# Keys and values of a fused attention layer: the fifth products on half the rows each, and weight chunks issued ahead of the turning transfers

## The chip, the cores and the metric

One core of one Trainium2 chip runs the whole kernel. The metric is the device time of one execution in microseconds; lower is better. A core has five instruction streams that matter here: TensorE (PE in the profile, with its weight loads as PEld), VectorE (DVE), ScalarE (ACT), GpSimd (POOL) and SyncE (SP), which here only issues DMA transfers. They meet at semaphores.

## The reference, cut to what matters

```
h  = tokenizer(x)                      # sines and cosines times W, joined with txt: 8 batches x 640 rows x 192
xn = layernorm(h)
k  = xn @ Wk ; v = xn @ Wv             # 192 -> 12 heads x 64
kf = concat(relu(k), relu(-k))         # per head, 128 features
kv = einsum('bhnd,bhnm->bhdm', kf, v)  # per batch and head, summed over the 640 rows
...                                    # queries, attention with kv, fusing product Wf (3072 x 768), Wo
h  = h + attention ; h = h + soft_experts(layernorm(h))
```

Every float32 product is built from bfloat16 halves: a value is its high half plus its low half, and a product is high by high, high by low and low by high.

## The kernel before, in words

The program runs in five stages, each a block with an end at which all engines meet: `tokenizer`, `attention_weights`, `keys_and_values`, `attend`, `soft_experts`. The change lies in the class `KeyInputs`, in `attention_weights` and `keys_and_values`, and with one transfer in `attend`.

The 5,120 rows of h are 40 tiles of 128 rows, 5 to a batch. For each tile, DVE normalizes 192 columns (L349), ACT copies the high half to `x_halves` (L353), DVE subtracts for the low half in two instructions (L356 and L357), and SP turns the three blocks of 128 columns by one DMA transpose into a slot of `x_turned` (L362). The blocks are: columns 0 to 127 high; columns 128 to 191 high over their low half; columns 0 to 127 low. So block 1 holds two things in its 128 rows: rows 0 to 63 are the high half of the last 64 columns, rows 64 to 127 their low half. The weights hold the last 64 rows of Wk and Wv twice, in rows 0 to 63 and 64 to 127.

`keys_and_values` makes, for each tile and each half of the heads (`hf`), keys and values of 384 columns each, by five matmuls for keys and then five for values (L642 to L646), into two banks. The fifth, L646, multiplies block 1 by the low weights. The last one of values releases ACT, which takes the positive part (L691), the negative part (L692) and the high half of values (L693). DVE and POOL subtract for the low halves of the features (L738 on DVE, L785 on POOL), DVE for the low half of values (L741). PE then adds 18 small matmuls (L658, six heads by three) to the sums `ps_kv`. PE's order is written out: project half hf of tile t, then accumulate half hf of tile t-1. `project` waits for L692 and L741 of the same half one tile earlier; `accumulate` waits for L738, L785, L693 and L741 of its half.

The stage also splits the 24 chunks of the fusing weights Wf, three to a batch, in tiles t = 0, 1 and 2. A chunk is loaded by SP (L596) into one of two buffers of `ex_big`. ACT makes its high half (L715) after both halves of its tile's key features; POOL makes the low half in two pieces (L791), each behind the L785 of the same hf, and waits for L715 with the first. So in these tiles L785 of hf = 1 comes after L715. Chunks 0 and 2 of a batch use buffer 0, chunk 1 uses buffer 1; a load waits until POOL is through with the chunk before it in the buffer.

SP's queue is in order. In iteration n (tile n, t = n mod 5) it stores tile n+1 of `x_turned` to memory (`keep_x`, L611), then turns tile n+3 (`turn_x`, L362), which waits for the low half L357 that DVE makes at the end of tile n, and then loads: at t = 1 chunk 2 of this batch, at t = 4 chunks 0 and 1 of the next.

`attend` begins with some 20 small loads for the last stage (L1010 to L1024, counted by `ex_in`), reads the kept tiles (L999, L1000) and turns its outputs (L1031). DVE adds the bias `bf` at the end of each tile (L1257). `bf` is loaded by ACT in `attention_weights` (L415).

Of the kernel before, what the change touches and what calls it, by code (L numbers as in the profile page):

```python
# [6 lines left out]
F32 = mybir.dt.float32  # L7
# [318 lines left out]
class KeyInputs:  # L326
# [3 lines left out]

    LEAD = 3
# [3 lines left out]
    def __init__(self, nc, sb, sem, xn):  # L335
        self.nc = nc
        self.xn = xn
        self.xs = sb("x_halves", [P, 2, 3 * P], BF16)
        self.xt = sb("x_turned", [P, 4, 3, P], BF16)
        self.norm, self.high, self.low, self.kept = (sem("x_" + n) for n in ("norm", "high", "low", "kept"))  # L340
        self.turned = [sem(f"x_turned{n}") for n in range(4)]
# [10 lines left out]
    def high_half(self, x):  # L352
        self.nc.scalar.activation(self.xs[:, x, 0:DIM], self.xn[:, :], ACT.Copy).then_inc(self.high, 1)  # L353

    def low_half(self, x):
        self.nc.vector.tensor_tensor(self.xs[:, x, 2 * P:3 * P], self.xn[:, 0:P], self.xs[:, x, 0:P], ALU.subtract)  # L356
        self.nc.vector.tensor_tensor(self.xs[:, x, DIM:2 * P], self.xn[:, P:DIM], self.xs[:, x, P:DIM],  # L357
                                     ALU.subtract).then_inc(self.low, 1)
# [6 lines left out]
def attention_weights(nc, a, w, wq_t, kv_f, x, stats, h, ident):  # L365
# [6 lines left out]
    with ExitStack() as ctx:  # L372
# [23 lines left out]
        with nc.Block() as block:  # L396
            @block.sync
            def _(sp):
                sp.dma_start(wt[:, :, :], a['wt_diag']).then_inc(wt_in, 16)
                sp.dma_start(bias[TAIL:P, :], a['bias_rows']).then_inc(bias_in, 16)  # L400
                sp.dma_start(wo_f[:, :, :], a['wo']).then_inc(wo_in, 16)
                for n in range(x.LEAD):
                    sp.wait_ge(x.low, n + 1)
                    x.turn(sp, n)
                for n in range(x.LEAD):
                    sp.wait_ge(x.turned[n], 16)

            @block.scalar
            def _(act):
# [5 lines left out]
                act.dma_start(w['bf'][:, :], a['bf'].partition_broadcast(P)).then_inc(small_in, 16)  # L415
# [26 lines left out]
                act.wait_ge(small_in, 16 * 8)  # L442

            @block.gpsimd
            def _(pool):
# [10 lines left out]
                eps = w['eps'][:, 0:PART]  # L456
                nc.gpsimd.memset(w['half'][:, :], -0.5).then_inc(halved, 1)  # L457
# [26 lines left out]
            def _(dve):  # L484
# [39 lines left out]
                dve.wait_ge(small_in, 16 * 8)  # L524
# [5 lines left out]
def keys_and_values(nc, a, w, x, x_kept, wf_f, kv_hi, kv_lo, stats, h, ident):  # L530
# [11 lines left out]
    with ExitStack() as ctx:  # L542
# [46 lines left out]
        with nc.Block() as block:  # L589
            @block.sync  # L590
            def _(sp):
# [14 lines left out]
                def keep_x(n):  # L606
                    at, uses = x.place(n // x.PERIOD, n % x.PERIOD)
                    sp.wait_ge(x.turned[at], 16 * uses + 16)
                    if n:
                        sp.wait_ge(x.kept, 16 * n)  # L610
                    sp.dma_start(x_kept[n], x.xt[:, at].rearrange("p k n -> p (k n)")).then_inc(x.kept, 16)  # L611
# [18 lines left out]
            def _(pe):  # L630
                def project(b, t, hf, early):
# [7 lines left out]
                    for kv in range(2):  # L639
                        cols = slice(kv * INNER + hf * HC, kv * INNER + (hf + 1) * HC)  # L640
                        out = ps_p[:, hf, kv, 0:HC]
                        nc.tensor.matmul(out, x.xt[:, at, 0], w['kv_hi'][:, 0, cols], start=True, stop=False)  # L642
                        nc.tensor.matmul(out, x.xt[:, at, 0], w['kv_lo'][:, 0, cols], start=False, stop=False)
                        nc.tensor.matmul(out, x.xt[:, at, 2], w['kv_hi'][:, 0, cols], start=False, stop=False)
                        nc.tensor.matmul(out, x.xt[:, at, 1], w['kv_hi'][:, 1, cols], start=False, stop=False)
                        last = nc.tensor.matmul(out, x.xt[:, at, 1], w['kv_lo'][:, 1, cols], start=False, stop=True)  # L646
# [154 lines left out]
def expert_tiles(sb):  # L801

# [42 lines left out]
def attend(nc, a, ex, w, x_kept, shared, kv_hi, kv_lo, h, ident):  # L845
# [14 lines left out]
    with ExitStack() as ctx:  # L860
# [66 lines left out]
        def count(tile, k, n):  # L927

            return n * tile.t + k + 1
# [62 lines left out]
        with nc.Block() as block:  # L992
            @block.sync
            def _(sp):
# [208 lines left out]
            def _(dve):  # L1203
# [49 lines left out]
                def move_y(tile):  # L1253
                    dve.wait_ge(s["fused"], count(tile, NO - 1, NO))
# [30 lines left out]
                def slots_square():  # L1285
                    dve.wait_ge(s["ex_in"], 16 * 20)
# [634 lines left out]
def early_fusion_kernel(nc, a, out):  # L1921
    with ExitStack() as ctx:
# [14 lines left out]
        with ExitStack() as attn:  # L1937
            def sa(name, shape, dt):
                return attn.enter_context(nc.sbuf_tensor(name, shape, dt))
# [5 lines left out]
                 'betaf': sa("betaf", [P, INNER // P], F32), 'bf': sa("bf", [P, INNER], F32),  # L1945
# [8 lines left out]
            with ExitStack() as keys:  # L1954
                x = KeyInputs(nc, lambda *v: keys.enter_context(nc.sbuf_tensor(*v)),
                              lambda name: keys.enter_context(nc.semaphore(name)), ex['xn'])
# [73 lines left out]
```

## Time and profile before

| | |
|---|---|
| time, median of 3 runs | 2398.43 us (2396.47 to 2402.49) |
| the profiled execution: its own time | 2402.28 us |
| its span, first to last instruction | 2400.6 us |
| mean granted TensorE clock | 0.977 |
| tokenizer | 0 to about 470 us |
| attention_weights | about 470 to 505.6 us |
| keys_and_values | 505.6 to about 722.6 us |
| attend | about 723 to 2340 us |
| soft_experts | the rest |

Busy time of PE counts each matmul from its start to its modelled end. Matmuls overlap: one of 384 columns is shown with 326 ns and the next one starts 162 ns after it, so the distance between starts is PE's pace. The clock column is the granted TensorE clock as a share of full speed.

### The profile page before, as it was taken

Reading aid. Unit: us, or ns where it says so; the run is one execution under the profiler, and the core shown is the slowest. Engines: PE = TensorE matmul, PEld = TensorE weight load, DVE = VectorE, ACT = ScalarE, POOL = GpSimd, SP = SyncE. Lnnn points to the kernel's source line nnn. Section 1 sums busy time; section 2 is a strip of 40 time slices with the busy share of each in tenths; the row PEclk is TensorE's granted clock in tenths of the full one; section 3 lists DMA queues with packets and bytes.
Section 4 is the critical chain, followed back from the end, with each engine's and each line's share of the span. In section 5 each row is a group of like instructions: output and inputs, shape, how many; then the busy total and the mean of one; then the engine's idle time right before and its main releaser. Section 6 shows DMA issues by size and latency. Waiting matters only on the chain. (4 is left out here: it accounts for less than half of the span.)

```text
span 2400.6 us, 58403 instructions
## 1 busy us (share of the span) xinstructions
PE 2270.0 (95%) x20906; PEld 1552.0 (65%) x20906; DVE 1998.1 (83%) x3021; ACT 1836.3 (76%) x2812; POOL 1286.2 (54%) x1253
## 2 busy tenths in 40 slices
PE   5999999978887999999999999999999999999976
PEld 3777777655554666666666666666666666666654
DVE  7999999876767888888888888888888888888855
ACT  6767677556667888888888888888888888888853
POOL 0000000056666776777777767676767767676760
PEclk9999999989998999999999999999999999999987
DMA  6412111122322222222222222222222222222212
GB/s 148 132 41 56 43 39 39 36 60 76 85 71 37 45 41 43 41 43 41 43 42 44 43 44 43 41 43 41 43 41 43 42 45 43 43 41 43 42 32 67
DMA packets 306607, 121.75 MB, mean 51 GB/s; under 512 B 280244, under 2 KB 297140, under 8 KB 306228
## 3 DMA queue, kind: packets, MB, share of 16 engines
q1 hardware_dynamic: 305396, 120.47, 23.4%
q8 instruction: 36, 0.59, 0.1%
q10 hardware_dynamic: 1152, 0.51, 0.1%
q14 instruction: 23, 0.19, 0.0%
HBM read 46.21 MB, written 7.86 MB: 23 GB/s over the span
## 5 line engine op out<-in xcount | busy, mean ns | idle before, releaser
L1162 ACT ACTIVATE phi<-ps_t,betat,gt 64x512 f32<-64x512 f32 (+1 forms) x1280 | 851.8, 665 | 17.4 <-PE ps_t L1061 0.2
L1093 PE MATMUL ps_y<-staging,o_turned 128*128 128x384 bf16 x3840 | 820.5, 326 | 0.0
L1377 POOL TENSOR_TENSOR phi_lo<-phi 128x512 bf16<-128x512 f32 x480 | 504.2, 1051 | 442.4 <-ACT phi L1162 442.4
L1093 PEld LDWEIGHTS ps_y<-staging,o_turned 128*128 128x128 bf16 x3840 | 361.8, 98 | 218.8 <-issue 0.2
L1093 PE MATMUL ps_y<-wf_lo,o_turned 128*128 128x384 bf16 x1920 | 469.2, 326 | 0.0
L1369 POOL TENSOR_TENSOR q_ssq<-q_ssq,half 128x8 f32<-128x8 f32 x240 | 418.2, 1743 | 18.8
L172 PE MATMUL acc<-w_b,feat 128*128 128x384 bf16 x1728 | 296.2, 331 | 33.1 <-ACT feat L223 27.4
L1250 DVE TENSOR_TENSOR o_halves<-o,o_halves 128x512 bf16<-128x512 f32 x240 | 192.2, 801 | 158.7 <-ACT o_halves L1172 158.6
L1152 ACT ACTIVATE shared<-shared 128x512 f32<-128x512 f32 x240 | 150.1, 626 | 176.6 <-DVE shared L1213 176.1
L1093 PEld LDWEIGHTS ps_y<-wf_lo,o_turned 128*128 128x128 bf16 x1920 | 187.9, 98 | 124.5 <-issue 0.3
L172 PEld LDWEIGHTS acc<-w_b,feat 128*128 128x128 bf16 x1728 | 168.3, 99 | 150.5 <-DVE w_b L298 23.7
L1213 DVE SCALAR_TENSOR_TENSOR shared<-q_sum,shared 128x512 f32<-128x512 f32 x240 | 260.8, 1087 | 1.4
L457 POOL MEMSET half<- 128x40 f32 x1 | 0.1, 131 | 468.7 <-POOLq L112 468.7
L284 DVE TENSOR_TENSOR f_low<-feat 128x4608 bf16<-128x4608 f32 x48 | 237.7, 4951 | 0.0
L1227 DVE TENSOR_TENSOR z<-shared,q_ssq 128x512 f32<-128x512 f32 x240 | 228.1, 950 | 0.6 <-POOL q_ssq L1369 0.6
L1078 PE MATMUL ps_o<-kvs_hi,phi 128*128 (+1 forms) x1920 | 209.0, 194 | 3.6
L1079 PE MATMUL ps_o<-kvs_lo,phi 128*128 (+1 forms) x1920 | 210.6, 194 | 0.0
L1080 PE MATMUL ps_o<-kvs_hi,phi_lo 128*128 (+1 forms) x1920 | 209.5, 193 | 0.0
L210 ACT ACTIVATE near<-xt,fr 128x2304 int32<-128x2304 f32 x48 | 106.6, 2220 | 130.5 <-DVE feat L268 121.9
L1078 PEld LDWEIGHTS ps_o<-kvs_hi,phi 128*128 128x128 bf16 x1920 | 177.7, 98 | 9.3 <-POOL phi_lo L1377 8.4
L1145 ACT ACTIVATE shared<-ps_a 128x512 f32<-128x512 f32 x240 | 143.5, 598 | 50.0 <-PE ps_a L1053 46.2
L1079 PEld LDWEIGHTS ps_o<-kvs_lo,phi 128*128 128x128 bf16 x1920 | 177.6, 98 | 2.8
(255 smaller groups left out, 4689.0 us busy)
## 6 DMA issues: line engine op xcount, KB each, us to landing
xt<-in_x_dram SPq DMA_DIRECT2D x32, 320.0 KB, 4.9
ex_big<-in_wf_dram SPq DMA_DIRECT2D x24, 384.0 KB, 3.6
xt<-in_x_dram SPq DMA_DIRECT2D x32, 256.0 KB, 5.4
x_kept<-x_turned SPq DMA_DIRECT2D x40, 96.0 KB, 2.0
shared<-x_kept SPq DMA_DIRECT2D x40, 96.0 KB, 1.9
o_turned<-o_halves SPq DMA_TRANSPOSE x240, 3.1
out_dram<-h SPq DMA_DIRECT2D x8, 480.0 KB, 5.1
staging<-in_wq_t_dram SPq DMA_DIRECT2D x1, 3072.0 KB, 12.8
```

The source lines that it names most:

```text
L172: last = nc.tensor.matmul(acc[:, u, t, 0:2 * DIM], high(p % RING)[:, k, t * P:(t + 1) * P], w_b[:, i, k, :], start=i == 0 and k == 0, stop ...
L284: nc.vector.tensor_tensor(low[:, r], feat[:, r], high(r), ALU.subtract).then_inc(low_ready, 1)
L1078: nc.tensor.matmul(out, ph, kv_hi[:, b, hd, :], start=c == 0, stop=False, skip_group_check=True)
L1079: nc.tensor.matmul(out, ph, kv_lo[:, b, hd, :], start=False, stop=False, skip_group_check=True)
L1080: last = nc.tensor.matmul(out, pl, kv_hi[:, b, hd, :], start=False, stop=c == PAIRS - 1, skip_group_check=True)
L1093: last = nc.tensor.matmul(ps_y[:, n, 0:HC], lhs, w[part][:, c, n * HC:(n + 1) * HC], start=c == 0 and lhs is hi and part == 'wf_hi', stop= ...
L1162: last = nc.scalar.activation(phi[sign * DH:(sign + 1) * DH, j % 2, a:b, head, :], ps_t[rows, a * P:b * P].rearrange("p (i n) -> p i n", n ...
L1213: nc.vector.scalar_tensor_tensor(out=q[:, j % RING], in0=total[:, j % 2].unsqueeze(2).broadcast_to([P, OCT, DH]), scalar=1.0 / DH, in1=q[: ...
L1227: nc.vector.tensor_tensor(z[:, j % 2], q[:, j % RING], ssq[:, j % 2].unsqueeze(2).broadcast_to([P, OCT, DH]), ALU.mult).then_inc(s["q_scal ...
L1250: nc.vector.tensor_tensor(oh[:, j % 2, 1], o[:, :, :, :].rearrange("p a h d -> p (a h d)"), oh[:, j % 2, 0], ALU.subtract).then_inc(s["o_l ...
L1369: nc.gpsimd.tensor_tensor(ssq[:, j % 2], ssq[:, j % 2], w['half'][:, 0:OCT], ALU.pow).then_inc(s["q_rstd"], 1)
L1377: nc.gpsimd.tensor_tensor(phi_lo[:, j % 2, :, head], phi[:, j % 2, :, head], phi_hi[:, j % 2, :, head], ALU.subtract).then_inc(s["phi_lo_d ...
```

## The change

- The turned input gets a fourth block. ACT writes the high half of the last 64 columns twice, by a second instruction: into the second half of a new block 0 and into the first half of block 2. The first half of block 0 is zero, set once by POOL at the start of `attention_weights`; SP waits for it (`cleared`). The three old blocks are now blocks 1, 2 and 3.
- The fifth product of keys uses rows 0 to 63 only (block 2), that of values rows 64 to 127 only (block 0). Both come after the other eight and stand next to each other in PE's order. The product of low by low half, which the old fifth product had in it, is left out.
- `x_halves` is no buffer of its own any more but lies in the memory of `bf`. So `bf` is loaded in `attend`, by SP, as one more of the loads of `ex_in`, and `move_y` of the first tile waits for it.
- SP loads a chunk of Wf at the start of an iteration, ahead of `keep_x` and `turn_x`: chunk 2 at t = 1, chunk 1 of the next batch at t = 3 and chunk 0 of the next batch at t = 4.

```diff
     def high_half(self, x):
-        self.nc.scalar.activation(self.xs[:, x, 0:DIM], self.xn[:, :], ACT.Copy).then_inc(self.high, 1)
+        self.nc.scalar.activation(self.xs[:, x, P:2 * P], self.xn[:, 0:P], ACT.Copy)
+        twice = self.xs[:, x, TAIL:TAIL + 2 * DIM].rearrange("p (k c) -> p k c", k=2)[:, :, 0:TAIL]
+        self.nc.scalar.activation(twice, self.xn[:, P:DIM].unsqueeze(1).broadcast_to([P, 2, TAIL]),
+                                  ACT.Copy).then_inc(self.high, 1)
...
-        self.xt = sb("x_turned", [P, 4, 3, P], BF16)
+        self.xt = sb("x_turned", [P, 4, 4, P], BF16)
...
+                sp.wait_ge(x.cleared, 1)
...
-                act.dma_start(w['bf'][:, :], a['bf'].partition_broadcast(P)).then_inc(small_in, 16)
...
+                nc.gpsimd.memset(x.xs[:, :, 0:TAIL], 0.0).then_inc(x.cleared, 1)
...
                 for n in range(TILES):
                     b, t = divmod(n, TPB)
+                    if t == 1:
+                        load(PER_BATCH * b + 2)
+                    if t >= 3 and b + 1 < BATCH:
+                        load(PER_BATCH * (b + 1) + 4 - t)
                     if n + 1 < TILES:
                         keep_x(n + 1)
                     if n + x.LEAD < TILES:
                         turn_x(n + x.LEAD)
-                    if t == 1:
-                        load(PER_BATCH * b + 2)
-                    if t == 4 and b + 1 < BATCH:
-                        for k in range(2):
-                            load(PER_BATCH * (b + 1) + k)
...
-                        nc.tensor.matmul(out, x.xt[:, at, 1], w['kv_hi'][:, 1, cols], start=False, stop=False)
-                        last = nc.tensor.matmul(out, x.xt[:, at, 1], w['kv_lo'][:, 1, cols], start=False, stop=True)
+                        nc.tensor.matmul(out, x.xt[:, at, 2], w['kv_hi'][:, 1, cols], start=False, stop=False)
+                    for kv, (rows, block_) in enumerate(((slice(0, TAIL), 2), (slice(TAIL, P), 0))):
+                        cols = slice(kv * INNER + hf * HC, kv * INNER + (hf + 1) * HC)
+                        last = nc.tensor.matmul(ps_p[:, hf, kv, 0:HC], x.xt[rows, at, block_],
+                                                w['kv_lo'][rows, 1, cols], start=False, stop=True)
                     last.then_inc(projected, 1)
...
+                sp.dma_start(w['bf'][:, :], a['bf'].partition_broadcast(P)).then_inc(s["ex_in"], 16)
                 sp.dma_start(ex['scale'][:, :], a['scale'].partition_broadcast(P)).then_inc(s["ex_in"], 16)
-                sp.wait_ge(s["ex_in"], 16 * 20)
+                sp.wait_ge(s["ex_in"], 16 * 21)
...
                 def move_y(tile):
+                    if isinstance(tile.t, int) and tile.t == 0:
+                        dve.wait_ge(s["ex_in"], 16 * 21)
```

## Rows read from the trace of the kernel before

**Rows 1.** Windows, two batches: busy (instructions) of PE, PEld, DVE, ACT, POOL; clock; DMA.
```profile
561.80:590.80 29.00, 23.70 (x280) 15.74 (x279) 17.34 (x37) 16.30 (x41) 15.97 (x17) 0.94 0.28 76
590.80:617.00 26.20, 22.70 (x284) 15.40 (x283) 19.23 (x39) 16.80 (x41) 15.98 (x17) 1.00 0.31 83
```

**Rows 2.** Waits of 505 to 725 us: total us, times, longest.
```profile
ACT kf L691 <- PE ps_p L646: 62.8, 51, 6.4
POOL wf_lo L791 <- ACT staging L715: 59.5, 17, 5.5
PEld ps_kv L658 <- POOL kf_lo L785: 30.1, 16, 3.8
ACT staging L715 <- DMA ex_big<-in_wf_dram: 23.1, 13, 3.0
```

**Rows 3.** Timeline of ACT, one batch.
```profile
589.46 0.49 ACT L691 ACTIVATE kf<-ps_p 128x384 f32<-128x384 f32 x1 [0.90 <-PE ps_p L646]
...
594.50 0.84 ACT L715 ACTIVATE staging<-ex_big 128x768 f32 x1 [1.36 <-DMA ex_big<-in_wf_dram]
...
605.49 0.84 ACT L715 ACTIVATE staging<-ex_big 128x768 f32 x1 [1.73 <-DMA ex_big<-in_wf_dram]
...
615.41 0.49 ACT L691 ACTIVATE kf<-ps_p 128x384 f32<-128x384 f32 x1 [0.68 <-PE ps_p L646]
```

**Rows 4.** Timeline of PE: the first matmuls of two halves.
```profile
562.66 0.33 PE L642 MATMUL ps_p<-shared,x_turned 128*128 128x384 bf16 x1
562.83 0.33 PE L643 MATMUL ps_p<-shared,x_turned 128*128 128x384 bf16 x1
...
564.84 0.33 PE L642 MATMUL ps_p<-shared,x_turned 128*128 128x384 bf16 x1
```

**Rows 5.** Timeline of SP, the same batch as in rows 3.
```profile
584.49 1.19 SPq L362 DMA_TRANSPOSE x_turned<-x_halves  x1
...
590.85 1.04 SPq L596 DMA_DIRECT2D ex_big<-in_wf_dram  x2
...
601.80 0.56 SPq L596 DMA_DIRECT2D ex_big<-in_wf_dram  x1
```

**Rows 6.** Timeline around tile 2 of that batch: POOL, DVE and PE.
```profile
597.52 0.91 POOL L791 TENSOR_TENSOR wf_lo<-ex_big,staging 128x384 f32 x1
...
601.27 1.26 DVE L738 TENSOR_TENSOR kf_lo<-kf 128x384 bf16<-128x384 f32 x1
602.46 0.55 DVE L741 TENSOR_TENSOR v_lo<-ps_p,v_hi 128x384 bf16<-128x384 f32 x1
603.15 0.32 PE L642 MATMUL ps_p<-shared,x_turned 128*128 128x384 bf16 x1 [0.45 <-ACT kf L692]
```

**Rows 7.** Timeline of PE in the last stage, matmuls on 32 rows.
```profile
2376.79 0.24 PE L1886 MATMUL ps_x<-yrows_lo,ct_hi 32*128 32x192 bf16 x2
2376.80 0.25 PE L1886 MATMUL ps_s<-yrows_lo,ct_hi 32*128 32x192 bf16 x2
...
2380.39 0.37 PE L1886 MATMUL ps_s<-yrows_hi,ct_lo 32*128 32x192 bf16 x2
2380.69 0.29 PEld L1865 LDWEIGHTS ps_c<-ex_big,hidden 128*128 128x128 f32 x1 [0.30 <-issue]
```

**Rows 8.** Timeline of ACT in attention_weights: pace of its instructions.
```profile
497.22 0.36 ACT L353 ACTIVATE x_halves<-ex_small 128x192 bf16<-128x192 f32 x1 [1.78 <-DVE ex_small L349]
497.49 0.37 ACT L419 ACTIVATE q_hi<-ps_f 128x256 bf16<-128x256 f32 x1
```

**Rows 9.** DMA issues of the page: KB each, median us to landing.
```profile
ex_big<-in_wf_dram SPq DMA_DIRECT2D x24, 384.0 KB, 3.6
```

**Rows 10.** DMA issues of 505 to 722 us.
```profile
x_turned<-x_halves SPq DMA_TRANSPOSE x37, 2.3
```

**Rows 11.** Timeline of SP at the start of attend.
```profile
734.59 0.42 SPq L1024 DMA_DIRECT2D ex_scale<-in_scale_dram  x1
744.79 0.35 SPq L999 DMA_DIRECT2D shared<-x_kept  x1
```

More of the change, by code:

```diff
@@ L333, with __init__ @@
     PERIOD = len(RING)
-    def __init__(self, nc, sb, sem, xn):
+    def __init__(self, nc, sb, sem, xn, xs):
         self.nc = nc
         self.xn = xn
-        self.xs = sb("x_halves", [P, 2, 3 * P], BF16)
-        self.xt = sb("x_turned", [P, 4, 3, P], BF16)
-        self.norm, self.high, self.low, self.kept = (sem("x_" + n) for n in ("norm", "high", "low", "kept"))
+        self.xs = xs
+        self.xt = sb("x_turned", [P, 4, 4, P], BF16)
+        self.norm, self.high, self.low, self.kept, self.cleared = (
+            sem("x_" + n) for n in ("norm", "high", "low", "kept", "cleared"))
         self.turned = [sem(f"x_turned{n}") for n in range(4)]
@@ L441, in _ @@
                         nc.scalar.activation(w['wo_hi'][:, :, :], wo_f[:, :, :], ACT.Copy).then_inc(wo_hi_done, 1)
-                act.wait_ge(small_in, 16 * 8)
+                act.wait_ge(small_in, 16 * 7)
             @block.gpsimd
@@ L522, in _ @@
                                                 ALU.subtract).then_inc(bias_split, 1)
-                dve.wait_ge(small_in, 16 * 8)
+                dve.wait_ge(small_in, 16 * 7)
                 for n, sign in (('gt', 0), ('betat', 1)):
@@ L610, in keep_x @@
                         sp.wait_ge(x.kept, 16 * n)
-                    sp.dma_start(x_kept[n], x.xt[:, at].rearrange("p k n -> p (k n)")).then_inc(x.kept, 16)
+                    sp.dma_start(x_kept[n], x.xt[:, at, 1:4].rearrange("p k n -> p (k n)")).then_inc(x.kept, 16)
                 load(0)
@@ L641, in project @@
                         out = ps_p[:, hf, kv, 0:HC]
-                        nc.tensor.matmul(out, x.xt[:, at, 0], w['kv_hi'][:, 0, cols], start=True, stop=False)
-                        nc.tensor.matmul(out, x.xt[:, at, 0], w['kv_lo'][:, 0, cols], start=False, stop=False)
-                        nc.tensor.matmul(out, x.xt[:, at, 2], w['kv_hi'][:, 0, cols], start=False, stop=False)
-                        nc.tensor.matmul(out, x.xt[:, at, 1], w['kv_hi'][:, 1, cols], start=False, stop=False)
-                        last = nc.tensor.matmul(out, x.xt[:, at, 1], w['kv_lo'][:, 1, cols], start=False, stop=True)
+                        nc.tensor.matmul(out, x.xt[:, at, 1], w['kv_hi'][:, 0, cols], start=True, stop=False)
+                        nc.tensor.matmul(out, x.xt[:, at, 1], w['kv_lo'][:, 0, cols], start=False, stop=False)
+                        nc.tensor.matmul(out, x.xt[:, at, 3], w['kv_hi'][:, 0, cols], start=False, stop=False)
+                        nc.tensor.matmul(out, x.xt[:, at, 2], w['kv_hi'][:, 1, cols], start=False, stop=False)
[3 more added lines that the diff above has]
+                                                w['kv_lo'][rows, 1, cols], start=False, stop=True)
                     last.then_inc(projected, 1)
@@ L1285, in slots_square @@
                 def slots_square():
-                    dve.wait_ge(s["ex_in"], 16 * 20)
+                    dve.wait_ge(s["ex_in"], 16 * 21)
                     nc.vector.tensor_tensor(ex['sl_sq'][:, :, :], ex['sl'][:, :, :], ex['sl'][:, :, :],
@@ L1955, in early_fusion_kernel @@
                 x = KeyInputs(nc, lambda *v: keys.enter_context(nc.sbuf_tensor(*v)),
-                              lambda name: keys.enter_context(nc.semaphore(name)), ex['xn'])
+                              lambda name: keys.enter_context(nc.semaphore(name)), ex['xn'],
+                              w['bf'].bitcast(BF16)[:, 0:8 * P].rearrange("p (k c) -> p k c", k=2))
                 attention_weights(nc, a, w, wq_t, kv_f, x, stats, h, ident)
```

6 lines of the change are left out of this document (3 added, 3 removed).

## The prediction

> **What bounds the kernel now.** I read the page first: PE is busy nearly everywhere, and the stage `keys_and_values` is one of the few stretches where its digits drop. It takes 217 us (505.6 to 722.6), 27 us a batch. The windows by batch then show that no engine is full there: in an undisturbed batch of 26.2 us PE is busy 22.7, DVE 19.2, ACT 16.8, POOL 16.0, at full clock [rows 1]. So the stage is held by waits. The rows of PE give its own need: one half of a tile takes 562.66 to 564.84, 2.18 us, made of ten matmuls at about 162 ns and 18 small ones for 0.56 us [rows 4]. Ten halves are 21.8 us; a batch takes 25.95 from its first L691 to that of the next [rows 3]. So some 4.2 us a batch are lost to waits.
>
> The list of waits names the chain [rows 2]. ACT waits 23.1 us in 13 waits for chunks of Wf. POOL waits 59.5 us for L715, the ACT copy of a chunk. PE's loads for L658 wait 30.1 us for POOL's L785, which stands behind that copy in POOL's order. The ACT waits for PE (62.8 us) are its normal slack; PE has none of that kind. The timeline shows where the loads come late. ACT wants chunk 0 at 593.14 and gets it at 594.50; it wants chunk 2 at 603.76 and gets it at 605.49 [rows 3]. SP had issued them at 590.85 and 601.80, each some 3.7 us before its use [rows 3, 5], and 3.6 us is what such a load takes [rows 9]. In SP's queue they stand behind a turning transfer that waits for the end of the tile.
>
> A second limit sits behind it. In tile 2 DVE's L738 takes 1.26 us, L741 of the same size 0.55; POOL, which works at the same time, is the likely reason. So the low half of values is done at 603.01 (602.46 plus 0.55), and PE starts its next half at 603.15 after 0.45 us of idle time [rows 6]. The row names L692 there, but L741 is the other wait of `project` and ended last. No load has to do with these 0.45 us.
>
> **The change part by part.**
>
> *Loads ahead.* Chunk 0 of a batch now goes out at the start of iteration t = 4, right behind the turning transfer of t = 3: that ended at 585.68 (584.49 plus 1.19), against 590.85 [rows 5]. Five microseconds earlier where 1.4 are missing: the wait goes. Chunk 1 goes two tiles before its use: it stays hidden. Chunk 2 is the thin one. It moves to the start of iteration t = 1, but must wait for POOL's second piece of chunk 0, which ended at 598.43 (597.52 plus 0.91), 3.1 us after ACT's copy of chunk 0 (594.50 plus 0.84) [rows 3, 6]. With the copy 1.4 us earlier that is 597.1; plus 3.7 is 600.8. ACT will want it at about 601.7 (603.76 less the 1.4 and some 0.7 of faster pace) [rows 3]. Hidden with 0.9 us to spare. While SP waits for POOL here, the store and the turn of that iteration stand behind it; the turn waits for the end of tile 1 anyway, which comes later than 597.1. Nothing is late.
>
> Gain: the 23.1 us [rows 2] lie on the path, since POOL's L785 and so PE stand behind them. The long stalls also cost clock: the batch of 29.0 us reads 0.94 instead of 1.00, which is 0.06 x 29 = 1.7 us of PE at full rate [rows 1]. It had the longest wait, 3.0 us [rows 2], and I give 3 us to it and its like. What the wait hid comes out in part: the POOL order (copy, first piece, L785, each about 1 us) leaves PE short some 0.3 to 0.7 us in chunk tiles. I take -25 us, with -18 and -30 as ends.
>
> *Fifth products side by side.* Per half, one slot of 162 ns goes [rows 4] if the two run at the same time. For that the trace has a near row: in the last stage four matmuls on 32 rows each start within 0.01 us and the next four come 0.09 us later, the time of 192 columns once [rows 7]. So 80 x 0.162 = 13 us of PE time. PE sets the pace in some six of the ten halves of a batch; in the chunk tiles DVE and POOL do [rows 6]. I take -7.5 us, ends -13 and, if they don't overlap, 0.
>
> *The border between whole and half array.* Before has no such border with PE busy on both sides at full clock. The nearest: after the last 32-row matmul at 2380.39 the next weight load starts at 2380.69, at half clock, where the matmul itself streams 0.16 [rows 7]. At most 0.14 us, and that includes a semaphore. Lower end 0; upper end per half is two borders at a matmul's tail, 0.326 less 0.162 each, 0.33 us [rows 4]. I take 0.03 per half, half of it on the path: +1 us; upper end +18 (there PE's pace of 2.35 covers the other chains).
>
> The Trainium skill (TensorEngine Tiling (Array Packing), Key Properties) says that a change of the tiling mode drains TensorE, and each half now has two. By that rule the sum is the drain rival below; the last stage's rows lean against it, since that weight load starts before the modelled end of the matmul (2380.39 plus 0.37), but they are one case.
>
> *The doubled high half.* ACT's instruction on 192 columns is followed by the next after 0.27 us [rows 8]. Two of 128 columns take between 0.36 (by columns) and 0.54 (no shorter at all); I take 0.45. That is +0.18 us a tile, 7.2 us of ACT in all. Cover: ACT's waits for PE, 62.8 us [rows 2]. Without cover it is 7.2. In tiles 0 and 1, where a chunk copy and a store of the sums also stand, ACT is nearly full; in `attention_weights` the first three come in a chain. +1 us, ends 0 and +4.
>
> *The fourth block.* The transfer of three blocks lands in 2.3 us [rows 10]; a third more is at most 3.1. It has two tiles until ACT and PE ask for it: nothing, except behind the last of the first three: +0.2. The clearing on POOL and SP's wait for it come long before the first low half: nothing. Storing three of the four blocks moves the same bytes. DVE's two low-half instructions keep their sizes.
>
> *The bias.* ACT issues one load fewer before its first work, when it waits for PE: nothing. SP issues one more, of the size of a chunk's load, behind 734.59. That is 0.6 us and a landing of some 3.6 [rows 9], done by 739; SP next works at 744.79 [rows 11]. Nothing. DVE asks for it at the end of the first tile, far later.
>
> Sum: -25 - 7.5 + 1 + 1 + 0.2 = -30.3 us. The profiled execution took 2402.3 (span 2400.6 plus 1.7), so it would give 2372; the median of the runs is 2398.4, 3.9 lower, and gives **2368**. As a check by batches: PE's own 20.2 us (ten times 2.02) plus some 2.2 of chains (0.4 to 0.7 in each chunk tile [rows 6]) is 22.4; eight of them and the 8 us of start and tail (217 less eight batches of 26.1) are 187 instead of 217. The same 30.
>
> **The rivals.**
>
> *Drain.* Both borders empty the array, +0.33 less 0.162 per half: PE's pace 2.35 us, 23.5 a batch, plus 0.4 of chains; 8 x 23.9 + 8 = 199, 18 us less than 217: **2381**. For it: two borders a half. Against: rows 7.
>
> *One after the other.* The halves don't overlap and the border is free: the loads alone, -25 + 2: **2375**. Against: the side-by-side starts of rows 7, though those are 32-row pieces.
>
> *PE sets the pace throughout.* POOL and DVE keep up: 20.4 a batch, 8 x 20.4 + 8 = 171: -46, **2353**. Against: the slow L738 [rows 6].
>
> *The wait moves.* SP, now waiting for POOL ahead of store and turn, or a chunk 2 that lands late, keeps most of the waits: a gain of 5 to 10 us, **2390**. For it: only 0.9 us to spare.
>
> *Slower.* The fifth products run one after the other and each of the three changes of rows (whole, lower, upper, whole) empties the array and loads its weights in the open: 0.164 plus 0.098 for the load, 0.79 per half. PE's pace is 2.97, a batch 29.7, the stage 246: +29, **2427**. It decides from a loss of 0.4 us per half on, which eats the 30 us of the rest. Against: the weight loads of rows 7 go ahead of the matmuls there.
>
> **How the numbers follow.** Chances: forecast 0.50, drain 0.17, one after the other 0.12, PE throughout 0.10, wait moves 0.06, slower 0.05. A measurement here tells 0.3%, 7.2 us, from no change (the three runs span 6 us). Only the last two cases reach towards no change: part of the wait case gives same. Faster 0.93, same 0.03, slower 0.04. The range holds the forecast with its ends of the load term (-18 and -30), the drain, one after the other, and up to PE throughout: 2352 to 2386, which leaves out the wait case, the slower one and little more.
>
> **What the profile after would show.** Right: no wait of ACT L715 for the transfer, or under 3 us in all; the two fifth matmuls of a half starting within 0.02 us, and the next L658 about 0.16 us later; the distance of first matmuls near 2.02 us in tiles 3 and 4; batches of about 22.4 us with PE's waits for POOL and DVE left in tiles 0 to 2; two ACT instructions 0.22 us apart per tile; the first o_turned transfer as far behind the start of `attend` as now. Drain: the L658 behind the fifth products starts over 0.3 us after them. Wait moves: ACT still waits for chunk 2, or PE for `x_turned`. The prediction is wrong if a batch takes under 21 or over 24.5 us, or if the rest of the kernel moves by more than 3 us.

## The result, and the profile after

The changed kernel took 2384.36 us (median of 4 runs, 2383.16 to 2384.71) beside 2400.46 for the kernel before (4 runs). The ratio is 0.9933, with a 95% interval from 0.9916 to 0.9951. It is faster, but by half of what was forecast: the forecast, 2368 from 2398.4, is a ratio of 0.987. The profiled execution took 2384.16 us, its span is 2382.4, its mean clock 0.979.

The whole gain lies where it was looked for. A clean measure of the stage is the time from the first to the last of its 80 starts of ACT's positive part. Before, it runs from 509.11 to 718.94 us, 209.8 us. After, the first and the last are:

```profile
509.16 0.49 ACT L700 ACTIVATE kf<-ps_p 128x384 f32<-128x384 f32 x1 [6.25 <-PE ps_p L654]
...
700.82 0.49 ACT L700 ACTIVATE kf<-ps_p 128x384 f32<-128x384 f32 x1 [0.97 <-PE ps_p L654]
```

That is 191.7 us, 18.2 less. The rest of the span is the same (2190.8 and 2190.7 us). I call this time **the stage** below. It tells more than the whole time: over all kernels of this study the rest of the span varies between 2186 and 2192 us from one execution to the next, while the stage of the changed kernel, profiled twice, came to 191.7 and 191.1. Every other kernel has one profile, so I read nothing into differences of the stage below 1 us.

The list of waits of the stage after (505 to 706 us; total us, times, longest), the counterpart of [rows 2]:

```profile
ACT kf L700 <- PE ps_p L654: 61.4, 69, 6.3
POOL kf_lo L794 <- ACT kf L701: 41.9, 29, 12.3
POOL wf_lo L800 <- ACT staging L724: 37.7, 22, 3.2
...
PEld ps_p L654 <- issue: 26.0, 80, 0.6
...
PE ps_p L648 <- DVE v_lo L750: 6.2, 5, 1.5
PEld ps_kv L667 <- POOL kf_lo L794: 6.1, 15, 1.2
```

ACT's 23.1 us for the chunks are gone, no such row is left. PE's weight loads wait 6.1 us for POOL instead of 30.1. Two rows are new or larger: the load for the fifth products (L654) stands 0.32 us in each of the 80 halves with nothing to wait for, and PE waits longer for DVE's low half of values (L750). In the kernel before, the same list (505 to 725 us) has for that wait:

```profile
PE ps_p L642 <- DVE v_lo L741: 3.0, 5, 1.7
```

The timeline of SP and of ACT for the same batch as in [rows 3, 5] shows the loads ahead of their use:

```profile
589.56 0.34 SPq L603 DMA_DIRECT2D ex_big<-in_wf_dram  x1
597.47 0.56 SPq L603 DMA_DIRECT2D ex_big<-in_wf_dram  x1
```
```profile
581.74 0.49 ACT L700 ACTIVATE kf<-ps_p 128x384 f32<-128x384 f32 x1 [0.80 <-PE ps_p L654]
...
585.50 0.85 ACT L724 ACTIVATE staging<-ex_big 128x768 f32 x1
...
594.97 0.85 ACT L724 ACTIVATE staging<-ex_big 128x768 f32 x1
...
605.98 0.49 ACT L700 ACTIVATE kf<-ps_p 128x384 f32<-128x384 f32 x1 [0.58 <-PE ps_p L654]
```

Both copies L724, of chunk 0 and of chunk 2, start without a wait. The load at 589.56 is chunk 2 of this batch and the copy at 594.97 its use: 5.4 us, where 3.6 are needed. This batch takes 24.24 us (581.74 to 605.98), where the forecast had 22.4 and had named 24.5 as the point from which it is wrong. The seven distances from batch to batch are 23.5 to 25.3 us, mean 24.46, and three of them are over 24.5; before, they have a mean of 26.35. The windows of two batches (columns as in [rows 1]):

```profile
533.00:556.50 23.50, 22.59 (x287) 13.57 (x284) 17.88 (x37) 17.28 (x46) 16.17 (x16) 1.00 0.53 101
581.70:606.00 24.30, 22.99 (x287) 13.82 (x285) 19.86 (x37) 17.52 (x46) 15.57 (x16) 1.00 0.39 94
```

The clock is at its full level in both. The slower batch has 2 us more of DVE at the same number of instructions (37): DVE's instructions themselves got longer in it.

PE around the fifth products of one half, to be held against [rows 4]:

```profile
589.37 0.32 PE L648 MATMUL ps_p<-shared,x_turned 128*128 128x384 bf16 x1
...
590.34 0.33 PE L650 MATMUL ps_p<-shared,x_turned 128*128 128x384 bf16 x1
590.50 0.33 PE L651 MATMUL ps_p<-shared,x_turned 128*128 128x384 bf16 x1
590.76 0.34 PE L654 MATMUL ps_p<-shared,x_turned 64*128 64x384 bf16 x2
591.03 0.20 PE L667 MATMUL ps_kv<-v_hi,kf 128*128 128x65 bf16 x1
...
591.59 0.33 PE L648 MATMUL ps_p<-shared,x_turned 128*128 128x384 bf16 x1
```
```profile
590.34 0.10 PEld L651 LDWEIGHTS ps_p<-shared,x_turned 128*128 128x128 bf16 x1
590.76 0.10 PEld L654 LDWEIGHTS ps_p<-shared,x_turned 64*128 64x128 bf16 x2 [0.32 <-issue]
591.03 0.10 PEld L667 LDWEIGHTS ps_kv<-v_hi,kf 128*128 128x128 bf16 x1 [0.17 <-issue]
```

The two fifth products do run side by side: one row, x2, 0.34 us, where one matmul alone is shown with 0.33. But from L651 to L654 it is 0.26 us and from L654 to L667 0.27, where a full matmul is followed by the next after 0.16. So each change between whole and half array costs 0.10 us. Two of them are 0.21 us a half; the saved slot is 0.16. A half takes 2.22 us (589.37 to 591.59) instead of 2.18; the forecast had 2.02. The weight loads behave differently too: L651's starts a whole matmul ahead of its own (590.34 for 590.50), L654's and L667's start only with their matmul. What fills the 0.10 us the rows don't settle. An array that empties would look like this, and so would a weight load, itself 0.10 us long, that is no longer hidden behind the matmul before it.

### The profile page after: what moved, and what is told of

It reads as the page before. It is cut to its first block and busy times, and to the rows that moved or that the text cites. A ratio compares the mean times of both kernels' runs of the same rounds, so it can differ in the third digit from the quotient of the medians.

```text
span 2382.4 us, 58446 instructions
## 1 busy us (share of the span) xinstructions
PE 2267.4 (95%) x20906; PEld 1537.5 (65%) x20906; DVE 2006.6 (84%) x3021; ACT 1842.7 (77%) x2852; POOL 1285.5 (54%) x1254
## 3 DMA queue, kind: packets, MB, share of 16 engines
q1 hardware_dynamic: 310660, 122.17, 24.5%
## 5 line engine op out<-in xcount | busy, mean ns | idle before, releaser
L1163 ACT ACTIVATE shared<-shared 128x512 f32<-128x512 f32 x240 | 150.2, 626 | 176.9 <-DVE shared L1224 176.4
L172 PEld LDWEIGHTS acc<-w_b,feat 128*128 128x128 bf16 x1728 | 167.8, 99 | 151.2 <-DVE w_b L298 24.4
```

Of the source, the lines that this page charges most:

```text
L172: last = nc.tensor.matmul(acc[:, u, t, 0:2 * DIM], high(p % RING)[:, k, t * P:(t + 1) * P], w_b[:, i, k, :], start=i == 0 and k == 0, stop ...
```

## The experiments

Each ratio is to the kernel before, run beside it on the same chip, with its 95% interval. "Stage" is the distance defined above; 209.8 before, 191.7 and 191.1 changed. A "half" is the time from one half's first matmul to the next one's where PE waits for nothing.

| kernel | time, us | ratio | stage, us | half, us |
|---|---|---|---|---|
| e1_loads_only | 2380.83 | 0.9925 [0.9911, 0.9938] | 190.9 | 2.18 |
| e2_fifths_only | 2399.30 | 1.0007 [0.9997, 1.0017] | 207.1 | 2.23 |
| e3_whole_fifths | 2381.70 | 0.9925 [0.9912, 0.9939] | 190.6 | 2.18 |
| e4_apart | 2396.69 | 0.9990 [0.9981, 1.0000] | 204.5 | 2.60 |
| e5_pool_order | 2372.88 | 0.9902 [0.9886, 0.9917] | 183.5 | 2.18 |
| e6_no_low_wf | 2362.65 | 0.9861 [0.9846, 0.9876] | 173.5 | 2.18 |
| e7_changed_no_low_wf | 2368.28 | 0.9883 [0.9868, 0.9898] | 176.4 | 2.23 |
| changed_again | 2381.41 | 0.9941 [0.9927, 0.9954] | 191.1 | 2.23 |
| e8_spread | 2378.84 | 0.9921 [0.9907, 0.9934] | 188.3 | 2.18 |
| e9_spread_and_order | 2379.18 | 0.9922 [0.9909, 0.9936] | 187.4 | 2.18 |
| e10_changed_pool_order | 2380.24 | 0.9924 [0.9911, 0.9938] | 188.8 | 2.23 |
| e11_nine_products | 2373.15 | 0.9910 [0.9894, 0.9927] | 183.5 | 2.02 |

### One part of the change at a time

**e1_loads_only** is the kernel before with nothing but the new place of the loads:

```diff
                 for n in range(TILES):
                     b, t = divmod(n, TPB)
+                    if t == 1:
+                        load(PER_BATCH * b + 2)
+                    if t >= 3 and b + 1 < BATCH:
+                        load(PER_BATCH * (b + 1) + 4 - t)
...
-                    if t == 1:
-                        load(PER_BATCH * b + 2)
-                    if t == 4 and b + 1 < BATCH:
-                        for k in range(2):
-                            load(PER_BATCH * (b + 1) + k)
```

> The kernel before with nothing changed but the order of SP's queue (the loads of the Wf chunks ahead of store and turn). Theory (borders): in the changed kernel each border between matmuls on 128 rows and on 64 rows costs PE 0.10 us, so the pair of fifth products saves 0.162 us and costs 0.21, a net loss of 0.05 us per half. Then this run has PE's pace at 2.18 us per half instead of 2.23, batches of some 23.8 us, and ends 1 to 5 us before the changed kernel: 2380 to 2383. Rival (chains): the fifth products gain their 0.162 us and the miss lies in the chains over POOL, DVE and the doubled ACT instruction; then this run is slower than the changed kernel where PE sets the pace: 2388 to 2392.

**e2_fifths_only** is the changed kernel with this edit taken back.

> The changed kernel with SP's queue in the old order (the fifth products, the fourth block, the doubled ACT instruction and the moved bias alone). Borders: PE's pace 2.23 us against 2.18, partly hidden behind the waits for chunks: 2400 to 2405, no faster than before. Chains: 7 us faster than before, 2393.

**e3_whole_fifths** is the changed kernel with its two fifth products in the same place, but on all 128 rows of block 2: no border between whole and half array, nothing side by side, and everything else of the change (fourth block, doubled high half, bias) in it.

```diff
-                    for kv, (rows, block_) in enumerate(((slice(0, TAIL), 2), (slice(TAIL, P), 0))):
+                    for kv, (rows, block_) in enumerate(((slice(0, P), 2), (slice(0, P), 2))):
```

> The changed kernel with both fifth products on all 128 rows of block 2, still last and next to each other; the layout, the doubled ACT instruction, the loads ahead and the bias as changed. This takes away both borders and the side by side at once. Borders: PE's pace 2.18 us, 1 to 5 us faster than the changed kernel, and within 1.5 us of the run with the loads alone, since the ACT instruction and the fourth block are hidden. Chains: 7 us slower than the changed kernel; if the doubled ACT instruction is what costs, 3 us or more above the run with the loads alone.

**e4_apart** keeps the two on half the rows but puts each right behind its own four products, so they can't run side by side and each half has four borders.

> The changed kernel with the fifth product of keys right after the other four of keys and that of values after those of values: each on 64 rows and alone between matmuls on 128 rows. Four borders a half instead of two, and nothing side by side. Borders: per half 4 x 0.10 + 2 x 0.162 + 8 x 0.162 + 0.56 = 2.58 us, 0.35 more than changed; 80 halves are 28 us, less some that chains cover: 2405 to 2413. Chains (borders free): 2.18 us per half, 2388 to 2392.

The loads alone give a stage of 190.9, and the changed kernel has 191.7 and 191.1. So the new place of the loads is the whole of the gain, and the fifth products as they are here give nothing. Without the loads ahead (e2) their time is within the noise of no change (1.0007). e2's stage is 2.7 us shorter than before's, but 2.4 of that lie in one batch, the third, which takes 29.25 us before and 26.80 in e2. There the profile of before has a stretch at half clock, which e2 has not (windows, columns as in [rows 1], before and e2):

```profile
570.00:573.00 3.00, 3.00 (x26) 1.82 (x27) 2.92 (x5) 1.40 (x4) 3.00 (x4) 0.57 0.05 15
```
```profile
570.00:573.00 3.00, 3.00 (x35) 1.64 (x32) 2.70 (x5) 1.35 (x4) 3.00 (x4) 1.00 0.06 13
```

So that part is most likely clock and not the fifth products. e3 has the stage of e1: the fourth block, the doubled instruction and the bias cost nothing that can be measured.

Of these expectations, those of e1 and e3 for the time held; e1's batch is 24.4 us and not 23.8. e2 ends just below its range (2399.3 for 2400 to 2405) and e4 far below its own (2396.7 for 2405 to 2413): its halves are as long as expected, but the stage is 13 us longer than the changed kernel's and not 28, since slower halves leave DVE and POOL more time.

e4 gives the price of a border without anything else in it. A border in its timeline of PE:

```profile
601.39 0.33 PE L651 MATMUL ps_p<-shared,x_turned 128*128 128x384 bf16 x1
601.65 0.33 PE L653 MATMUL ps_p<-shared,x_turned 64*128 64x384 bf16 x1
601.91 0.34 PE L648 MATMUL ps_p<-shared,x_turned 128*128 128x384 bf16 x1
```

Twice 0.26 us again, 0.10 more than streaming. Four borders make a half of 2.60 us, (2.60 - 2.18) / 4 = 0.105 each. With that the changed kernel's half is 2.18 - 0.162 + 2 x 0.105 = 2.23, which is what it shows. e3 in the same place, without a border:

```profile
601.13 0.33 PE L651 MATMUL ps_p<-shared,x_turned 128*128 128x384 bf16 x1
601.29 0.49 PE L654 MATMUL ps_p<-shared,x_turned 128*128 128x384 bf16 x2
601.62 0.19 PE L667 MATMUL ps_kv<-v_hi,kf 128*128 128x65 bf16 x1
```

0.16 us to the first, and two whole slots for the pair. e4 says one thing more. Its batches are ten times 2.60, 26.0 us, and the chunk tiles add nothing: when PE is this slow, DVE and POOL are always done in time.

### What holds the batches at 24.5 us

With the loads ahead a batch of e1 takes 24.4 us and PE's own need is 21.8. The 2.6 us between are not the loads any more. The timeline of the changed kernel in tiles 1 and 2 of the batch shown above, POOL, DVE and PE:

```profile
597.73 0.91 POOL L800 TENSOR_TENSOR wf_lo<-ex_big,staging 128x384 f32 x1
598.60 1.14 POOL L794 TENSOR_TENSOR kf_lo<-kf 128x384 bf16<-128x384 f32 x1
600.01 1.21 POOL L794 TENSOR_TENSOR kf_lo<-kf 128x384 bf16<-128x384 f32 x1 [0.27 <-ACT kf L701]
```
```profile
597.75 1.31 DVE L747 TENSOR_TENSOR kf_lo<-kf 128x384 bf16<-128x384 f32 x1 [0.66 <-ACT kf L701]
598.98 0.55 DVE L750 TENSOR_TENSOR v_lo<-ps_p,v_hi 128x384 bf16<-128x384 f32 x1
599.98 0.56 DVE L747 TENSOR_TENSOR kf_lo<-kf 128x384 bf16<-128x384 f32 x1 [0.45 <-ACT kf L701]
```
```profile
597.13 0.33 PE L648 MATMUL ps_p<-shared,x_turned 128*128 128x384 bf16 x1
...
599.67 0.32 PE L648 MATMUL ps_p<-shared,x_turned 128*128 128x384 bf16 x1
...
601.90 0.33 PE L648 MATMUL ps_p<-shared,x_turned 128*128 128x384 bf16 x1
```

POOL's L800 starts at 597.73, DVE's L747 0.02 us later. L747 takes 1.31 us instead of 0.56 and ends at 599.06, which is 0.42 behind the end of L800 (598.64). It pushes the end of L750 to 599.53, and PE's next half starts at 599.67. That half came 2.54 us behind the one before, the next again 2.23. At 599.98 the order is the other way round: DVE starts first and takes its 0.56; POOL's L794, 0.03 us later, takes 1.21 instead of 0.84. So the two don't slow each other by a share. The one that starts first runs at its own speed and the other stands until it is nearly through.

I held this against all of the stage: 75 instructions of DVE of this kind (L747, L362, L363) start while one of POOL's runs for at least 0.1 us more. 71 of them end 0.11 to 0.16 us before "POOL's end plus their own free duration" (0.56, 0.28 and 0.21 us). Of the other four, three stand beside a row in which two of POOL's are merged, and one started within 0.03 us of POOL's. L750, which reads one of its inputs from PSUM, has a mean of 0.551 us and is never longer than 0.56. L352, the normalizing step with only one large input in SBUF, isn't spared: it takes 0.38 us at least and up to 1.05, and every long one stands beside a busy POOL.

The Trainium skill (SBUF — State Buffer, Who interferes with whom) says that DVE and GpSimd share a pair of ports as an exclusive lock, that a DVE instruction with two SBUF inputs needs it against a GpSimd instruction that reads SBUF, and that the one which starts first has it for its whole length. The trace agrees, down to the L750 that is spared; L352, which is not of that kind, shows that two inputs in SBUF are not the only case.

**e6_no_low_wf** and **e7_changed_no_low_wf** take nearly all of POOL's chunk work away, from e1 and from the changed kernel. They leave out the low half of Wf but for 16 of 384 columns of each piece; the rest is set to zero at the start of `attention_weights`:

```diff
-                                cols = slice(hf * HC, (hf + 1) * HC)
+                                cols = slice(hf * HC, hf * HC + 16)
```

> The kernel with the loads alone, with POOL making only 16 of 384 columns of each piece of a chunk's low half; the low weights of Wf are otherwise zero, set once at the start of attention_weights, which may cost a few us there. The low half of Wf is thus left out of the fusing product. Theory (DVE slowed by POOL): DVE's mean for the negative features' low part falls from about 0.8 to 0.65 us or less, PE's waits for the low half of values go, batches fall from 24.5 to 22 to 22.6 us; 2362 to 2370. If the limit is something else (ACT, SP, PE), batches stay above 24.

> The changed kernel with the same left out as in the run before it. With the chains out of the way PE alone sets the pace, and the price of the fifth products should show in full: borders theory 2.23 us against 2.18 per half, batches 0.4 to 0.5 us longer than in the run before it, 3 to 4 us in all, 2365 to 2374. Borders free: 5 to 13 us faster than the run before it.

**e5_pool_order** is e1 with another order on POOL: both low halves of the tile's features first, then both pieces of the chunk.

```diff
-                            if t < PER_BATCH:
-                                c = PER_BATCH * b + t
...
+                        if t < PER_BATCH:
+                            c = PER_BATCH * b + t
+                            pool.wait_ge(wf_hi_ready, c + 1)
+                            for hf in range(2):
```

> The kernel with the loads alone, with POOL's order changed: in a chunk tile both halves of the positive features' low part come first and the two pieces of the chunk's low half after them, so no feature work stands behind the ACT copy of the chunk. Question: what holds a batch at 24.5 us where PE needs 21.8. Theory (DVE slowed by POOL): DVE's subtractions with both inputs in SBUF take up to twice or four times as long while POOL works, whatever POOL's order, so the gain is small: 0 to 4 us, 2377 to 2381. Rival (POOL's order): PE is short of features because they stand behind the copy: batches of 22.5 us, 2362 to 2368.

**changed_again** is the changed kernel once more, on the same chip as these three.

> The changed kernel once more, to compare it with the loads alone (2380.8 us, ratio 0.9925 to before) against the same runs of before. Borders: ratio 0.9935 to 0.9945, 2383 to 2385. If the fifth products gained, it would be under 0.9915.

Without the chunk pieces the stage falls from 190.9 to 173.5 us (e6) and a batch to 22.0 (mean), close to PE's own 21.8. So POOL's chunk work is worth 17 us of this stage, and it is nearly all that stood between e1 and PE's own need. DVE's low half of features, by groups of instructions (busy us, mean ns), in the changed kernel, in e1, in e5 and in e6:

```profile
L747 DVE TENSOR_TENSOR kf_lo<-kf 128x384 bf16<-128x384 f32 x80 | 64.9, 811 | 34.8 <-ACT kf L701 34.5
```
```profile
L737 DVE TENSOR_TENSOR kf_lo<-kf 128x384 bf16<-128x384 f32 x80 | 64.4, 805 | 31.9 <-ACT kf L691 31.6
```
```profile
L737 DVE TENSOR_TENSOR kf_lo<-kf 128x384 bf16<-128x384 f32 x80 | 58.0, 725 | 34.7 <-ACT kf L691 34.1
```
```profile
L738 DVE TENSOR_TENSOR kf_lo<-kf 128x384 bf16<-128x384 f32 x80 | 47.6, 595 | 41.5 <-ACT kf L692 41.3
```

The same group of the kernel before has this mean:

```profile
L738 DVE TENSOR_TENSOR kf_lo<-kf 128x384 bf16<-128x384 f32 x80 | 56.4, 705 | 61.2 <-ACT kf L692 59.8 <-PE ps_kv L658 0.8
```

The loads ahead raised it from 705 to 805 ns: L737 takes 8 us more in all. That is one place where a part of their gain went. The waits of e1 show who pays, PE for DVE's low half of values, 13.3 us, where it was 3.0 before:

```profile
PE ps_p L641 <- DVE v_lo L740: 13.3, 19, 1.7
```

In all 19 of these waits the L737 just ahead of L740 took 1.17 to 1.20 us instead of 0.56. One of the longest, PE at 599.69, has these rows of DVE and PE:

```profile
597.90 1.17 DVE L737 TENSOR_TENSOR kf_lo<-kf 128x384 bf16<-128x384 f32 x1
599.00 0.55 DVE L740 TENSOR_TENSOR v_lo<-ps_p,v_hi 128x384 bf16<-128x384 f32 x1
```
```profile
599.69 0.32 PE L641 MATMUL ps_p<-shared,x_turned 128*128 128x384 bf16 x1 [1.66 <-DVE v_lo L740]
```

Beside these 13.3 us PE's matmuls wait only 1.6 us for POOL's L784, and its weight loads 4.4. So in e1 the lock shows in PE's waits far more than POOL's own time does.

e5's time, 2372.88, lies between its theory (2377 to 2381) and the rival (2362 to 2368), so neither held as written: the stage is 183.5, 7.3 less than e1's, and the order does matter to the lock. It brings DVE's mean down to 725 ns, and PE's wait for DVE falls by 7.4 us to this:

```profile
PE ps_p L641 <- DVE v_lo L740: 5.9, 11, 0.8
```

e5 leaves nothing out and beats both kernels: 0.9902 beside 0.9941 for the changed kernel on the same chip (2371.30 to 2373.11 us against 2380.80 to 2382.40).

e7 against e6 is the price of the fifth products with nothing else in the way: 176.4 against 173.5 us of stage, and 2368.28 against 2362.65 in time, in ranges that don't touch. 80 halves at 0.05 us are 4. The times of e6 and e7 lie in their expected ranges, and so does changed_again's ratio; the batches of e7 are 0.35 us longer than e6's.

### Other ways round POOL, and the pace alone

**e8_spread** is e1 with the chunks in tiles 0, 1 and 3 instead of 0, 1 and 2. **e9_spread_and_order** is that with the order of e5, **e10_changed_pool_order** the changed kernel with the order of e5.

> The kernel with the loads alone, with the third chunk of a batch split in tile 3 instead of tile 2 (tiles 0, 1, 3). POOL's and ACT's work is the same. Theory (DVE slowed by POOL, over three tiles in a row): DVE and POOL catch up in tile 2, batches of 23.7 to 24.2 us instead of 24.6, 3 to 7 us faster than the loads alone: ratio 0.990 to 0.991. Rival: the sum of DVE's slow instructions sets the batch wherever they lie: no change, 0.9925.

> The loads ahead, POOL's new order and the chunks in tiles 0, 1 and 3 together, fifth products as in the kernel before. If the two limits behind the loads (POOL's order, DVE's slow instructions in three tiles in a row) are separate: batches of 22.6 to 23.0 us, ratio 0.987 to 0.989, the fastest full kernel here. If the order has already taken what the spreading could give: 0.990, as with the order alone.

> The changed kernel with POOL's new order. With less of the chains left, the price of the borders shows more than in the changed kernel itself: 2 to 5 us above the loads with POOL's new order (ratio 0.9902), that is 0.991 to 0.9925, batches of 23.4 to 23.8 us. Borders free: 0.989 or less.

Of the spread's two expectations the first is undecided and the second was missed. Alone (e8) it takes 2.6 us from the stage (188.3) and its batches (mean 23.98 us) are those of the theory, but the time doesn't tell it from nothing (0.9921 and 0.9925). With the order (e9) it loses 3.9 us of what the order had given (187.4 against 183.5). The mean of DVE's low half is 882 ns in e8 and 759 in e9, above the 725 of e5, so the lock isn't met less often. But in e9 it isn't what PE pays: its matmuls wait 6.2 us for DVE's low half of values, as in e5 (5.9). What grew is their wait for ACT's negative part, from 2.3 us in e5 to this in e9:

```profile
PE ps_p L642 <- ACT kf L692: 6.4, 14, 0.5
```

That is 4.1 us more, as much as the 3.9 that were lost. What keeps ACT there I have not settled.

e10's stage is 188.8, 2.3 to 2.9 less than the changed kernel's but 5.3 more than e5's. With the order mended the fifth products cost more than without it (0.2 to 0.8 us of stage against e1), and also more than the 4 us that 80 halves at 0.05 us can explain. DVE's mean is 759 ns in e10 and 725 in e5, so the longer halves may bring a worse meeting with POOL; that isn't shown.

**e11_nine_products** asks what PE's pace alone is worth. It is e1 without the fifth product of keys (that term is left out of the keys): nine matmuls on all rows, no border.

```diff
-                        nc.tensor.matmul(out, x.xt[:, at, 1], w['kv_hi'][:, 1, cols], start=False, stop=False)
-                        last = nc.tensor.matmul(out, x.xt[:, at, 1], w['kv_lo'][:, 1, cols], start=False, stop=True)
+                        nc.tensor.matmul(out, x.xt[:, at, 1], w['kv_hi'][:, 1, cols], start=False, stop=kv == 0)
+                        if kv:
+                            last = nc.tensor.matmul(out, x.xt[:, at, 1], w['kv_lo'][:, 1, cols], start=False, stop=True)
```

> The kernel with the loads alone, without the fifth product of keys: nine matmuls a half instead of ten, all on 128 rows, so the product of keys' last 64 columns with the low weights is left out. It gives PE exactly the pace of the prediction, 2.02 us per half, with no border. Prediction's sum (PE sets the pace in six of ten halves, batches of 22.4 us): 7 us and more faster than the loads alone, ratio 0.987 to 0.9895. Theory by now (with the loads ahead, the chains over POOL and DVE hold a batch near 24.4 us whatever PE needs below that): batches of 23.9 to 24.4 us, 0 to 3 us faster, ratio 0.991 to 0.9925.

Its stage:

```profile
508.14 0.49 ACT L691 ACTIVATE kf<-ps_p 128x384 f32<-128x384 f32 x1 [6.03 <-PE ps_p L646]
...
691.66 0.49 ACT L691 ACTIVATE kf<-ps_p 128x384 f32<-128x384 f32 x1 [0.75 <-PE ps_p L646]
```

183.5 us, 7.3 less than e1, with batches of 23.4 us: between the two theories, which had 22.4 and 23.9 to 24.4. The whole time has it smaller (0.9910 against 0.9925, 3.6 us, with intervals of 4 us to either side), so the two agree within what they can tell. I take the stage, but the 7.3 rests on one profile of each kernel.

## Why the prediction was half right

The sum of the forecast, term by term, against the stage:

| term | forecast, us | measured, us | from |
|---|---|---|---|
| loads ahead | -25 (-18 to -30) | -19.0 | e1 less before |
| a slot of 0.162 us less per half | -7.5 (-13 to 0) | -7.3 | e11 less e1 |
| borders | +1 (0 to +18) | +7.9 | changed (mean of two) less e11 |
| doubled instruction, fourth block, bias | +1.2 (0 to +4) | -0.2 | e3 less e1 |
| all | -30.3 | -18.2 and -18.7 | changed less before |

The row of the borders is a difference of two kernels and holds the row below it too; that one is nothing. By its making it closes the sum, so that the sum comes out is no proof of it; its own support is the 0.21 us read from the rows of PE, and e4.

Two terms failed, both in size: the borders (7 us of the 12 that are missing) and the loads ahead (6 us).

**The border was the step with the wrong value.** "I take 0.03 per half, half of it on the path" should have been 0.21 per half. Half on the path fits: 80 x 0.21 / 2 is 8.4. The reading of [rows 7] failed. It had the weight load behind the last 32-row matmul start before that matmul's modelled end, and took this as a sign against a drain. That sign tells nothing: in the changed kernel too the weight loads behind both borders start before the modelled end of the matmul ahead of them (590.76 for a matmul shown from 590.50 to 590.83). The distance there, 0.30 us at half clock, is 0.14 more than the streaming of 0.16; the text itself called 0.14 an upper bound and then took a value near the lower end. The Trainium skill's rule (TensorEngine Tiling (Array Packing), Key Properties), that a change of the mode drains TensorE, was the better guide: the trace agrees that every border has a price, here 0.10 us; that it is the draining, and not the weight load in the open, isn't shown. The drain rival was right that both borders cost PE, and too dear in its price, 0.164 a border instead of 0.10. Its time, 2381, is nearer to the result (by ratio 0.9933 to 0.9941, 2382 to 2384 on the scale of the forecast) than the forecast's own. Its sign in the profile, the next L658 over 0.3 us behind the fifth products, did not appear, since 0.27 lies below that line.

**The loads' term was at its small end.** The wait of 23.1 us went, wholly, and chunk 2 did not become late. Before to e1 the stage fell by 19.0 us, and e2 to the changed kernel, with the fifth products in both, by 15.7 (mean of two). The difference of 3 us is, but for 0.9, in the one batch of before at half clock. e2 keeps the waits for chunks (21.8 us of ACT) and has no half clock there, so the 3 us that the sum added for clock were in this profile of before, but that the waits cause them isn't shown. The larger miss is what stood behind the wait: a batch of e1 is 2.6 us over PE's own need, 0.9 for each chunk tile. The forecast saw the slow L738 in [rows 6] and named POOL as likely; it allowed 0.3 to 0.7 us in each chunk tile. It did not ask whether the loads ahead would make the two meet more often, and they do (705 to 805 ns over 80 instructions). That POOL's chunk pieces hold e1 above PE's need is shown by e6. e6 removes POOL's own time as well as the lock, so it doesn't divide the 17 us between the two; but PE's waits in e1 do in part, 13.3 us behind a lengthened L737 against 1.6 for POOL, and so does e5, which takes off 7.3 us with all of POOL's work still there.

**What held.** The two fifth products do run at once, so "one after the other" fell. The doubled instruction, the fourth block and the bias are free: ACT's two instructions start 0.20 us apart (594.57 and 594.77, 0.32 us each), and ACT still waits 61.4 us for PE. The rest of the kernel moved by 0.1 us. The share of a shorter half that reaches the end, six of ten, came out as 7.3 / 13 = 0.56.

**The other rivals.** PE sets the pace throughout: no, in chunk tiles DVE and POOL still do; but e4 shows that PE does set it once its half is 2.60. The wait moves: SP now waits 18.1 us for POOL's L800, and nothing behind it is late. Slower: it needed a loss of 0.4 us per half, and the loss is 0.05.

The range had the time near its upper end, since it reached to the drain. The mean batch of 24.46 us lies just under the 24.5 that was to prove it wrong, and the 2.22 us from half to half is far from the 2.02 named as the sign of being right. The bound of 24.5 was drawn too far from 22.4 to tell the two apart.

Three things stay open. Whether a border's 0.10 us is an emptying array or an unhidden weight load was not separated. Side-by-side products without a border couldn't be had in this loop, as each half ends with matmuls on the whole array; e11 is only a stand-in for their pace. And why ACT comes later in e9, where the spread chunks undo half of the order's gain, was not found.

## What to carry to other kernels

A pair of matmuls on half of the rows saves one slot and costs two borders. Work out both from a trace with matmuls of that length: here 0.16 us saved against 0.21 paid, per pair. By these numbers, as an estimate, a loop needs two or more pairs between its borders before it gains (2 x 0.162 against 0.21); no run here had two.

Where DVE and POOL both subtract from operands in SBUF, look at which starts first, and not only at how busy each is. A duration of one instruction that varies twofold in a group is the sign. Here an order on POOL that puts what PE waits for first was worth 7 us, as much as dropping the tenth matmul of each half.

When a wait is taken away, ask what else used it: the gap in POOL's work had been keeping it out of DVE's way.

## What the hardware showed that I had not expected

- A change between 128-row and 64-row matmuls costs 0.10 us at full clock, in each direction, with matmuls of 384 columns (0.26 and 0.27 us from start to start instead of 0.16). The weights of the matmul behind a border are loaded only when it starts, not during the one before.
- DVE with two inputs in SBUF and POOL nearly take turns by whole instructions: 0.56 us becomes up to 1.31 (128x384), 0.28 up to 0.94 (128x128), 0.21 up to 0.95 (128x64); POOL's 0.84 becomes 1.12 to 1.27 when DVE is ahead of it. DVE's 0.38 us with one large input (L352) also becomes up to 1.05.
